# First experts' up products and attention's scores made from two float32r parts instead of three bf16 parts, on row tiles of the array

## The reference, cut to what matters

```python
xn = layernorm(x)
x  = x + rwkv6_attention(xn) + first_experts(xn)
xn = layernorm(x)
x  = x + causal_attention(xn) + second_experts(xn)

def first_experts(x):          # 8 heads of 16 channels, 16 experts of 64 units, top 2
    t = (x @ Wm + bm).reshape(-1, 16)
    w = softmax(t @ expert_emb); topw, topi = top_k(w, 2)
    hmid = gelu(einsum('td,edi->tei', t, W1) + b1)      # "up": contraction over 16
    eo = einsum('tei,eio->teo', hmid, W2) + b2          # "down"
    return combine(eo, topw, topi) @ Wo + bo

def causal_attention(x):       # 16 heads of 8 channels, one shared key and value head
    latent = x @ Wc_down
    q = latent @ Wq_up;  k, v = split(latent @ Wkv_up)
    att = einsum('bthd,bsd->bhts', q, k) / sqrt(8)      # "score": contraction over 8
    return softmax(causal(att)) @ v @ Wc_proj
```

## Time and profile before

| | before |
|---|---|
| median of 3 runs | 1351.73 us (1351.6 to 1356.91) |
| span of the profiled execution | 1317.6 us |
| PE busy | 1206.5 us, 92% |
| DVE busy | 1050.7 us, 80% |
| ACT busy | 891.2 us, 68% |
| POOL busy | 482.3 us, 37% |

### The profile page before, as it was taken

One profiled execution on the slowest core, in us unless ns is written; L12 is line 12 of the kernel. 1 busy time (PEld: TensorE's weight loads), 2 busy tenths in 40 slices (PEclk: granted clock), 3 DMA queues, 4 the chain that ended last, 5 costly groups with the idle time before them and its releaser, 6 DMA issues. The chain is left out here.

```text
span 1317.6 us, 28397 instructions
## 1 busy us (share of the span) xinstructions
PE 1206.5 (92%) x11172; PEld 593.3 (45%) x11172; DVE 1050.7 (80%) x1954; ACT 891.2 (68%) x1246; POOL 482.3 (37%) x446
## 2 busy tenths in 40 slices
PE   6888998899988989798899999999899999999988
PEld 3333332333433323365555555555456544555434
DVE  4589789869898779769977799778787798787863
ACT  3668997898877888643266676666666666666666
POOL 3542554345514872320155511555025550000170
PEclk8889998999999999989999999999999999999999
DMA  6333322233332343248364544556335453233020
GB/s 224 116 117 125 106 94 101 92 109 101 100 103 94 111 132 106 93 118 233 106 183 136 174 122 117 151 139 157 87 101 160 133 142 89 72 82 105 19 64 28
DMA packets 129876, 152.88 MB, mean 116 GB/s; under 512 B 16048, under 2 KB 90800, under 8 KB 129616
## 3 DMA queue, kind: packets, MB, share of 16 engines
q1 hardware_dynamic: 111104, 127.50, 32.9%
q0 software_dynamic: 8192, 16.79, 4.3%
q10 hardware_dynamic: 10448, 6.77, 1.7%
HBM read 109.20 MB, written 41.81 MB: 115 GB/s over the span
## 5 line engine op out<-in xcount | busy, mean ns | idle before, releaser
L2887 ACT ACTIVATE ax_prob<-second_pair 128x1024 f32<-128x1024 f32 (+1 forms) x320 | 292.9, 939 | 146.4 <-PE second_pair L2840 94.4
L528 ACT ACTIVATE m_act_h<-first_pair,const 128x1024 f32<-128x1024 f32 x256 | 270.1, 1114 | 57.7 <-PE first_pair L482 44.1
L2764 DVE TENSOR_REDUCE am_top<-second_pair 128x2 f32<-128x1024 f32 (+1 forms) x192 | 222.9, 1175 | 38.6 <-PE second_pair L2718 25.5
L3019 POOL DMA_INDIRECT slot_tokens<-xn,mr_slots x128 | 124.0, 969 | 273.7 <-PE second_bank L1877 86.2
L3049 POOL DMA_INDIRECT m_back<-slot_results,mr_slots x128 | 122.2, 955 | 243.2 <-PE second_pair L2718 167.7
L482 PE MATMUL first_pair<-m_terms,w1s 96*128 96x512 bf16 x512 | 145.9, 391 | 19.6 <-ACT m_act_h L528 19.4
L2826 PE MATMUL ax_sums<-ax_prob,al_vs 128*32 128x512 f32 (+3 forms) x1536 | 161.2, 500 | 1.8 <-ACT ax_prob L2887 1.6
L494 PE MATMUL first_pair<-m_act_h,const 128*32 128x512 f32 x1024 | 130.4, 610 | 7.0 <-DVE m_prod L543 4.9
L582 POOL TENSOR_TENSOR m_both<-m_prod,m_both 128x512 f32<-128x512 f32 x64 | 86.7, 1371 | 123.8 <-DVE m_both L543 123.8
L2863 PE MATMUL second_pair<-al_qs,al_ks 51*128 51x512 bf16 (+3 forms) x768 | 115.9, 329 | 12.8 <-DVE am_top L2764 4.3
L2718 PE MATMUL second_pair<-al_ks,al_qs 48*128 48x512 bf16 (+3 forms) x768 | 116.2, 327 | 7.6 <-DVE am_top L2764 3.7
(11 more groups left out here) (396 smaller groups left out, 2515.1 us busy)
## 6 DMA issues: line engine op xcount, KB each, us to landing
m_wt<-in_experts SPq DMA_DIRECT2D x96, 384.0 KB
m_share<-shares SPq DMA_DIRECT2D x128, 256.0 KB
m_rows<-slot_tokens SPq DMA_DIRECT2D x60, 128.0 KB
slot_results<-m_y SPq DMA_DIRECT2D x60, 128.0 KB
stack<-mp_part SPq DMA_DIRECT2D x48, 128.0 KB
m_terms<-stack SPq DMA_DIRECT2D x64, 96.0 KB, 3.7
qstack<-ap_qpart SPq DMA_DIRECT2D x48, 128.0 KB
al_qs<-qstack SPq DMA_DIRECT2D x32, 192.0 KB, 3.9
```

The costliest lines, as they stand in the source:

```text
L528: A.activation(self.act_h[:, slot, :, :], banks.bank("up", n, ep)[:, :, :], ACT.Gelu, bias=self.w("b1", 4 * half + ep, 4 * half + ep + 1)) ...
L2764: V.tensor_reduce(into[:, 2 * a:2 * a + 2, at], tile[:, :, 0:n], AX, ALU.max, negate=True).then_inc(*banks.empties("max", i, m))
L2887: A.activation(dst, src, ACT.Exp, scale=SCALE).then_inc(*banks.empties("sum", i, u))
L3019: G.indirect_dma_start(self.tokens[g], bass.IndirectOffsetOnAxis(ap=self.route.slots[g][second][:, i:i + 1], axis=0), self.entry.zn(GC * g ...
```

## The change

**First experts.** The activations and the weights are split into two float32r parts (`hi` and `lo`). Four products of 16 rows are kept (TERMS = 4), so a head takes 64 rows, and the two heads of a use lie on the two 64-row halves of the array. The `mid` copy on ACT and one subtraction on POOL go for each tile, sends fall from 6 of 128 KB to 4 of 256 KB, and reads from 64 of 96 KB (6 slots) to 32 of 256 KB (2 slots). `lo` is written over `h`, so the next tile's `h` waits for the send.

**Attention.** Queries, keys and maxima are split into two float32r parts, of which three products are kept: 24 rows (26 with the maximum), so each of the four heads of a task has its own strip of 32 rows. A use is always two heads (strips 0, 1 or 2, 3), so a task has 24 uses in place of 20 in each of its two products. The masks are 32 rows deep: 8 matmuls for each diagonal use, of 128, 96, 64 and 32 columns on each of two strips. They come from DRAM ready in bf16, so five DVE casts go. Splits of the queries and keys fall from 3 DVE operations to 1 and from 2 ACT copies to 1, splits of the maxima from 4 DVE operations to 1. `turn` takes one bank in place of a pair. A task's queries take 4 DMAs in place of 2, its maxima 2 + 4 in place of 3 + 2, and a tile's queries and keys are sent with 6 DMAs in place of 12. The planner gets a model of two pairs of strips that work side by side and new costs. Its wished times are unchanged.

```diff
-TERMS = 6
-ACT_PARTS = (0, 0, 1, 1, 0, 2)
-WEIGHT_PARTS = (0, 1, 0, 1, 2, 0)
+TERMS = 4
+ACT_PARTS = (0, 1, 0, 1)
+WEIGHT_PARTS = (0, 0, 1, 1)
+Q_TERMS, Q_PARTS, K_PARTS = 3, (0, 0, 1), (0, 1, 0)
+STRIP = 32
...
-            a.wait_ge(self.lo_made, i)
+            a.wait_ge(self.parts_sent, i * 16 * TERMS)
...
-            yield FIRST["mid", i]
-            a.wait_ge(self.rest_made, i + 1)
-            A.activation(self.parts[1][:, :], self.h[:, :], ACT.Copy).then_inc(self.mid_made, 1)
...
-                    p = E.matmul(banks.bank("up", n, ep)[:, j, :], self.w1s[:, (4 * half + ep) * P:(4 * half + ep + 1) * P], self.terms[:, q % slots, :], start=True, stop=True)
+                    rows = slice(TERMS * FD * j, TERMS * FD * (j + 1))
+                    p = E.matmul(banks.bank("up", n, ep)[:, j, :], self.w1s[rows, (4 * half + ep) * P:(4 * half + ep + 1) * P].bitcast(F32R),
+                                 self.terms[rows, q % slots, :].bitcast(F32R), start=True, stop=True)
...
-            V.tensor_tensor(self.rest[0], self.q[c % 2], hi, ALU.subtract).then_inc(split, 1)
-            V.tensor_copy(mid, self.rest[0]).then_inc(split, 1)
-            V.tensor_tensor(lo, self.rest[0], mid, ALU.subtract).then_inc(split, 1)
+            V.tensor_tensor(lo.bitcast(F32R), banks.bank("q", c)[:, :], hi, ALU.subtract).then_inc(*banks.empties("q", c))
...
+    def strip(self, a, x, n=MROW):
+        first = STRIP * (2 * a + x)
+        return slice(first, first + n)
...
-                    for queries in range(2):
+                    for n32 in range(QUARTERS):
                         for x in range(2):
-                            p = self.forbid(banks.bank("max", i, m), x, queries, len(pairs) > 1, n - CH)
+                            p = self.forbid(banks.bank("max", i, m), a, x, n32, n - CH)
...
+    def forbid(self, tile, a, x, n32, off):
+        rows, first = self.loads.strip(a, x, STRIP), STRIP * n32
+        return self.k.nc.tensor.matmul(tile[:, x, off + first:off + CH], self.k.masks[rows, 0, n32, :], self.k.masks[rows, 1, n32, first:CH],
+                                       start=False, stop=True, skip_group_check=True)
```

More of the change, by code:

```diff
@@ L1958, in vector_key @@
         for c in range(NT):
             rows = self.rows(c)
[L1960 removed]
+            hi, lo = (k[rows, :] for k in self.k_parts)
             yield AT["split_k", c]
             v.wait_ge(self.k_made, c + 1)
[L1963 to L1964 removed]
             if c > 1:
                 self.all_sent(v, c - 2)
[L1967 removed]
@@ L1968, in vector_key, with vector_value @@
-            v.wait_ge(split, 3 * c + 1)
-            V.tensor_copy(mid, rest).then_inc(split, 1)
-            v.wait_ge(split, 3 * c + 2)
-            V.tensor_tensor(lo, rest, mid, ALU.subtract).then_inc(split, 1)
-    def vector_value(self):
+            V.tensor_tensor(lo.bitcast(F32R), banks.bank("k", c)[rows, :], hi, ALU.subtract).then_inc(*banks.empties("k", c))
+    def vector_value(self, loaded):
         V, v, banks = self.k.nc.vector, self.k.dve, self.banks
@@ L2020, in columns @@
     return TILE - max(0, blk * CH - th * TILE)
-WEIGHT_USES = [(m, pairs) for m in range(len(SUM_STEPS)) for pairs in pairs_with(columns(m))]
+WEIGHT_USES = [(m, a) for m in range(len(SUM_STEPS)) for a in PAIRS]
 LAST_USE = [max(u for u, (step, _) in enumerate(WEIGHT_USES) if step == m) for m in range(len(SUM_STEPS))]
@@ L2074, in __init__, with step @@
         self.last_fill, self.place, self.tenants = {}, {}, [[] for _ in range(banks)]
-    def step(self, engine, stream, key, wish, takes, *needs, lag=0.12, fills=0, use=None, uses=None, completes=None, frees=None, since=0.0, table=None, port=False):
+        self.strips = {}
+    def step(self, engine, stream, key, wish, takes, *needs, lag=0.12, fills=0, use=None, uses=None, completes=None, frees=None, since=0.0, table=None, port=False, strips=None):
+        self.strips[key] = strips
         assert key not in self.steps, key
@@ L2141, in run @@
             at[key] = start
+            if engine == "PE":
+                issued = start
+                strips_free = [start + takes if self.strips[key] in (None, n) else strips_free[n] for n in range(2)]
             engine_free[engine] = start + takes
@@ L2775, in scalar_turn @@
             a.wait_ge(*banks.full("turn", i))
-            a.wait_ge(self.split, 4 * i)
-            A.activation(self.rows[0:nr, :], banks.bank("turn", i)[0:nr, 0, 0:CH], ACT.Copy).then_inc(*banks.empties("turn", i))
+            a.wait_ge(self.sent[i % 2], 32 * (i // 2))
+            A.activation(self.parts[i % 2][0][0:nr, :].bitcast(F32R), banks.bank("turn", i)[0:nr, 0:CH], ACT.Copy).then_inc(self.hi_made, 1)
     def vector_turn(self):
@@ L2881, in scalar @@
                 a_.wait_ge(*banks.full("sum", i, u))
-                if len(pairs) > 1:
-                    src, dst = narrow(banks.bank("sum", i, u), TILE - off), self.prob[:, g % 3, :, off:TILE].rearrange("p (a x) n -> p a x n", x=2)
-                else:
-                    a, = pairs
-                    src, dst = banks.bank("sum", i, u)[:, :, off:TILE], self.prob[:, g % 3, 2 * a:2 * a + 2, off:TILE]
-                A.activation(dst, src, ACT.Exp, scale=SCALE).then_inc(*banks.empties("sum", i, u))
+                A.activation(self.prob[:, g % 3, 2 * a:2 * a + 2, off:TILE], banks.bank("sum", i, u)[:, :, off:TILE], ACT.Exp, scale=SCALE).then_inc(*banks.empties("sum", i, u))
     def scalar_y(self, start):
@@ L3458, in arrays @@
               ("b1", g0["b1"].reshape(EP, P).T), ("b2", g0["b2"].reshape(2, P).T), ("bo", col(g0["bo"]))]
-    for n in range(3):
-        parts.append((f"rows{n}", col(np.repeat(np.array([p == n for p in WEIGHT_PARTS], f32), FD))))
+    for n in range(2):
+        parts.append((f"rows{n}", col(np.tile(np.repeat(np.array([p == n for p in WEIGHT_PARTS], f32), FD), 2))))
     w2 = np.zeros((EP, 2, FI, 2, FD), f32)
```

378 lines of the change are left out of this document (158 added, 220 removed).

## The result

The change makes the kernel slower by a tenth. The median after is 1479.09 us (1475.15 to 1499.17, 5 runs), that of before beside it 1352.88 us; the ratio is 1.095 (95% interval 1.090 to 1.099). The forecast was 1341 us, in a range of 1308 to 1372: wrong in sign and outside the range.

A forecast was written before the change was run, and what follows sets the result against it. PE alone bounds the second stage's dense part; PE, DVE and ACT take turns in the first. Terms -25 - 2 - 6 + 22 = -11 give a 1306.6 us span, 1340.7 us with 34.1 around it, against 1351.7; range 1308 to 1372.

The forecast's parts named there:

- attention 16 us longer (22 less 6): Attention: dense part 22 us longer (masks 32, narrow scores 5, loads 5, overlap -20), projections 6 us shorter.
- the first stage 27 us shorter: First stage: 25 us from cheaper up products and 2 us from a shorter way to the first unit.
- The weight loads: Attention: slower float32r loads cost 5 us, mostly hidden behind streaming matmuls; 77 us if all the difference lay open.
- The narrow scores: Attention: 128 uses of 128 columns cost 5 us, between nothing at bf16's price and 30 us at float32's.
- The up products' 25 us: First stage: a use costs 0.215 us less, 55 us of PE over 256 uses; 25 us taken, bounds 0 and 55.
- Rival 3: The first stage does not move, since ACT and DVE have its length: total +14, 1366 us; chance 0.14.
- The clock: Whole kernel: read as at or near its upper level, 2.4 GHz, in nearly all slices; no term in the sum.
- Masks and overlap: Attention: mask groups take 0.15 us, 32 us more in all; uses side by side on strips save 20 us.
- a diagonal use hides nothing: Attention: matmuls go in order, so only the 256 uses off the diagonal can overlap, at most 56 us.
- The plain uses: Attention: uses off the diagonal run beside others on strips, saving 0.22 us each; 20 us taken, between 0 and 56.
- Projections and the first unit: Fewer DVE operations in attention's projections save 6 us (0 to 18); a shorter way to the first unit 2 (0 to 3.8).

The follow-up runs named there:

- att_only: The changed kernel with the first stage of the kernel before, so attention's part of the change alone; 1.0740 of before.
- att_bf16: Attention's part of the change alone, with the two parts of queries, keys and maxima in bf16 instead of float32r; 1.0190 of before.
- The bf16 parts: The first stage's part of the change alone, with both parts in bf16 instead of float32r; 1.0167 of before, against 1.0256 in float32r.
- before_replanned: The kernel before, instructions unchanged, with the planner's cost of an up use at 0.23 us in place of 0.44; 1.0204 of before.
- seven first-stage kernels: Kernels with the first stage's part of the change alone, in float32r or bf16, varying products issued, slots, planner costs or a wait; 1.0167 to 1.0328 of before.
- before_att_replanned: The kernel before, instructions unchanged, with attention's planner costs raised for narrow scores (0.06 to 0.11 us) and masks (0.08 to 0.17); 1.0142 of before.
- the products alone: TensorE alone running sections of such products; in attention's mix a round took 2.89 us on strips in bf16, 3.34 in float32r, 3.09 on halves.
- up_bf16_kept: First stage's change alone in bf16, three slots, planner costs and steps of before, and before's waits for h and the last send; 1.0247 of before.
- att_rowmask: Attention's part of the change alone, with masks of 128 rows, 2 products a use instead of 8 on strips; 1.1187 of before.

## Why the prediction was wrong

**The steps in the forecast's own terms.** It had attention 16 us longer (22 less 6) and the first stage 27 us shorter. Measured, attention's half costs 7.4 points, some 100 us, and the first stage's half 2.6 points, some 35 us.

**The weight loads are the step that failed most.** The forecast took 5 us for them, "but they start while an earlier matmul streams", with 77 us if all the difference lay open. The upper bound is what came: 76 to 86 us by the products at a steady clock, and 74 us by att_only against att_bf16, where loads and clock are together. The likely mechanism is this. The earlier products here are masks of 32 to 128 columns with weights of their own. Between two uses there are ten loads and little streaming, so that two loads of 192 ns have nothing to hide behind. The narrow scores, 5 us in the forecast, are part of it: 128 uses at 0.17 us in place of 0.07 make 13 us. In the first stage the loads do have long products ahead, but the float32 ones there are often on all rows: four up products after such a one hold PE for 0.67 us (500.90 to 501.57), two uses, where the forecast had 0.44. By the same measure they held it for 0.97 us in before (504.15 to 505.12). So a use is 0.15 us cheaper, not 0.215: an estimate of 38 us of PE saved in place of 55. The bf16 parts save 0.9 points there.

The Trainium skill, on the page "TensorE: Matmul & The Clock Gate", "Weight-path perf modes", has a fast load for 128 weights of any type but float32, and the forecast noted that it doesn't say how float32r counts. The runs do: 192 ns for float32r against 93 for bf16 on the same strips, so it counts as float32.

**The order was assumed to stay.** The up products' 25 us were argued "since the wished times that rank the streams stay as they are". The wishes did stay, but the planner's cost of a use, its kind of tile and the preparation's steps did not, and before_replanned shows that the cost alone, with unchanged instructions, costs 2.0%. What the shorter products themselves give was forecast at 25 of 55 us. None of the seven first-stage kernels shows a gain, but they stand in three plans, and none of them is the plan of before. So it is shown that another order can lose as much as the first stage lost, and not shown how its 35 us divide between order, clock and products. Rival 3 (the first stage does not move) had no term for the order either. Attention's costs changed as well; before_att_replanned makes it likely that most of att_bf16's 1.9 points are of this kind, but its order is another again, so this is argued, not shown.

**The clock was a constant in the sum.** Every duration was taken at the level of the trace before. It fell from 0.978 to 0.909. In the first stage it falls where TensorE has more gaps, with the change (0.90) or with another order alone (0.95 in before_replanned, against 0.99). In attention it was 0.93 over att_only's dense part and 1.00 over that of att_bf16.

**Masks and overlap.** The forecast had 0.15 us a group and 32 us more. In place a group of 8 stands some 0.18 us apart (1131.47 to 1131.65), and leaving all groups out won 58 us, at a somewhat lower clock (0.924 against 0.929), where those of before took 45 by the earlier trace rows. That step was right within its bounds. "The matmuls go in order, and masks start when their own scores have passed", so that a diagonal use hides nothing, was wrong for bf16 in the products alone, where masks hide under the next scores (0.24 us a use). The plain uses did what was forecast: in after, 70 uses start within 0.06 us of one on the other strips. At 0.22 us each that is 15 us, where the forecast had 20.

**Projections and the first unit** (6 and 2 us) are too small to be seen beside an order's 20 to 30 us; nothing here tells.

**Open.** How attention's 74 us divide between loads and clock: the products alone give all of it at a steady 2.4 GHz, while the kernels' clocks differ too, and TensorE was busy for 530 of 550 us where the clock was 0.93. By 145 against 30 us at half speed the clock alone could cost up to 58 us, as an estimate; why it falls there is not shown. What the first stage's change is worth in the order of before is open as well: the kernel to run is up_bf16_kept without the `TILES` entry, with its products issued once and twice. No version here beats the kernel before.

## What to carry to other kernels

Where a planner or a hand-tuned order places the work, price the new order as a term of its own: in this kernel three of three replannings of unchanged work lost 1.4 to 2.0%, about what the forecast promised for the shorter up products, and an edit's own worth is only seen with the order held. Compare the two orders step for step before calling one held: here a single entry in a table was enough to change it. A load that hides behind long products is in the open between short ones: count the loads between two uses, not only the columns. And before pricing a cut in one engine's work, ask whether its clock will stay where the gaps grow: TensorE's went from 0.99 to 0.95 in this first stage by the order alone.

## What the runs showed of the hardware

- Float32r weights load in 181 to 199 ns at the upper clock level, about as float32 ones do (193), bf16 ones in 91 to 99 ns, whether 24, 64 or 96 rows are filled. The products themselves stream within 6% of bf16's pace (0.230 against 0.217 us a pair on halves).
- With TensorE busy without a gap, the granted clock went to 1.2 GHz in the sections that used only two strips of 32 rows, in float32r (for 33 of 38 us) and in bf16 (36 of 39 us), and in none that used half of the rows or more, or four strips in turn. Strips mixed with products on all rows kept 2.4 GHz.
- In att_rowmask a float32r use of 384 columns on strips was followed by a product on all 128 rows after 0.38 us (after 0.28 by one on its own strips in after), and two such products of 128 columns by the next use on strips after 0.22 us. Eight short products on the strips took 0.18 us.
- Groups of runs of one and the same kernel differed by 2.7% between chips (1319 to 1355 us) at clocks of 0.975 and 0.967, and most of it lies in the second stage (768 against 789 us).
